# An order of its own for the first eight slots of an attention and feed-forward kernel

## The reference

```python
q, k, v = (x @ Wk.T + bk), (ctx @ Wk.T + bk), (ctx @ Wv.T + bv)      # per head
s  = q k' / sqrt(32)
p  = softmax(where(allow, s, -1e32));  cum = cumsum(p)
eff = clip(exp(sqrt(clip((total - cum) * |i - j|, 0)) * -softplus(gamma)), 1e-5, 1e5)
a  = softmax(where(allow, s * eff, -1e32)) @ v
x1 = layernorm(x + a @ Wo.T + bo)
out = layernorm(x1 + relu(x1 @ W1.T + b1) @ W2.T + b2)               # 512 -> 2048 -> 512
```

## Time and profile before

| | |
|---|---|
| median of 3 runs | 1585.5 us (1583.85 to 1588.65) |
| the profiled execution | 1583.35 us |
| its span, first to last instruction | 1581.6 us |
| busy | PE 1489.3, weight loads 1234.4, DVE 1129.6, ACT 1038.3, POOL 108.1 us |
| mean granted TensorE clock | 0.976 |
| moved by DMA | 334 MB, 211 GB/s |

### The profile page before, as it was taken

One profiled execution on the slowest core, in us unless ns is written; L12 is line 12 of the kernel. 1 busy time (PEld: TensorE's weight loads), 2 busy tenths in 40 slices (PEclk: granted clock), 3 DMA queues, 4 the chain that ended last, 5 costly groups with the idle time before them and its releaser, 6 DMA issues.

```text
span 1581.6 us, 34611 instructions
## 1 busy us (share of the span) xinstructions
PE 1489.3 (94%) x13056; PEld 1234.4 (78%) x13056; DVE 1129.6 (71%) x3843; ACT 1038.3 (66%) x2677; POOL 108.1 (7%) x96
## 2 busy tenths in 40 slices
PE   4577899999999999999999999999999999999897
PEld 3455788888888888888888888888888888887786
DVE  5788668687776868777686877768687776867433
ACT  2777666766666676666667666666766666676522
POOL 4000101000010100100010010101000000100000
PEclk8778999999999999999999999999999999999999
DMA  6775455565655556565555656555565655555676
GB/s 213 249 244 218 182 187 202 201 216 197 216 209 200 204 201 220 191 225 201 200 204 199 222 192 225 201 201 206 200 223 190 223 202 201 206 200 202 245 281 251
DMA packets 62773, 334.12 MB, mean 211 GB/s; under 512 B 8208, under 2 KB 8208, under 8 KB 29456
## 3 DMA queue, kind: packets, MB, share of 16 engines
q1 hardware_dynamic: 62608, 331.92, 58.9%
HBM read 306.72 MB, written 25.17 MB: 210 GB/s over the span
## 4 chain that ended last, share of the span: by engine, by line
PE 64%; DVE 24%; ACT 8%; issue 2%; POOL 1%; DMA 0%; SPq 0%; DVEq 0%; POOLq 0%; ACTq 0%
PE bank L199 18%; PE bank L200 16%; PE bank L201 16%; PE bank L385 7%; DVE w_sb L925 5%; DVE w_sb L913 5%; PE bank L399 4%; DVE w_sb L935 2%; DVE gz L921 2%; ACT w_sb L637 1%; ACT w_sb L639 1%; ACT w_sb L635 1%; DVE s_sb L901 1%; PE bank L419 1%; DVE rows L988 1%
## 5 line engine op out<-in xcount | busy, mean ns | idle before, releaser
L199 PE MATMUL bank<-xt_hi,w_ring 128*128 128x256 f32 x1024 | 296.9, 290 | 2.3 <-ACT h_sb L708 2.3
L201 PE MATMUL bank<-xt_hi,w_ring 128*128 128x256 f32 x1024 | 288.9, 282 | 0.0
L200 PE MATMUL bank<-xt_lo,w_ring 128*128 128x256 f32 x1024 | 288.6, 282 | 0.0
L901 DVE CUSTOM_DVE_ANT_0 s_sb<-bank,mask 128x256 f32<-128x256 f32 (+7 forms) x512 | 130.1, 304 | 184.0 <-PE bank L385 182.2
L658 ACT COPY pt_sb<-bank 128x512 f32<-128x512 f32 x192 | 111.9, 583 | 200.1 <-PE bank L399 200.1
L628 ACT ACTIVATE w_sb<-s_sb,nm 128x161 f32<-128x161 f32 (+7 forms) x512 | 164.3, 404 | 87.9 <-DVE nm L909 87.9
L199 PE MATMUL bank<-w_ring,h_hi 128*128 128x512 f32 x512 | 210.9, 412 | 9.6 <-DVE h_lo L1000 9.6
L648 ACT ACTIVATE p_sb<-w_sb,nm 128x32 f32<-128x32 f32 (+7 forms) x512 | 205.6, 405 | 0.0
L201 PE MATMUL bank<-w_ring,h_lo 128*128 128x512 f32 x512 | 203.2, 397 | 0.0
L200 PE MATMUL bank<-w_ring,h_hi 128*128 128x512 f32 x512 | 203.1, 397 | 0.0
L199 PEld LDWEIGHTS bank<-xt_hi,w_ring 128*128 128x128 f32 x1024 | 193.5, 189 | 9.1 <-issue 5.9
(11 more groups left out here) (120 smaller groups left out, 2961.3 us busy)
## 6 DMA issues: line engine op xcount, KB each, us to landing
w_ring<-w_split SPq DMA_DIRECT2D x256, 1024.0 KB, 4.9
w_split<-w_ring SPq DMA_DIRECT2D x32, 512.0 KB, 5.4
x_raw<-x_t SPq DMA_DIRECT2D x16, 512.0 KB, 4.0
c_raw<-ctx_t SPq DMA_DIRECT2D x16, 512.0 KB, 5.0
u_sb<-x_rows SPq DMA_DIRECT2D x16, 512.0 KB, 6.4
ring_raw<-w SPq DMA_DIRECT2D x32, 256.0 KB, 5.5
out<-rows SPq DMA_DIRECT2D x16, 512.0 KB, 6.9
wk_raw<-wk SPq DMA_DIRECT2D x1, 1024.0 KB, 4.8
```

The source lines that it names most:

```text
L199: nc.tensor.matmul(dst, a_hi, b_hi, start=start, stop=False)
L200: nc.tensor.matmul(dst, a_hi, b_lo, start=False, stop=False)
L201: return nc.tensor.matmul(dst, a_lo, b_hi, start=False, stop=stop)
L901: m = nc.vector.tensor_tensor_reduce(out=s_sb[:, c % 2, W_AT[b] + 1:W_AT[b] + 1 + WIDTH[b]], in0=s_bank[n % 2][:, at:at + WIDTH[b]], in1=m ...
```

## The change

The first eight slots (batches 0 and 1, steps 0 and 1 up to the start of step 2) get a function `first()` on every engine, with its own order; from step 2 on, `step` is as before. In `first()`:

- DVE empties all three parts of the scores of a slot before `decayed_scores` of the slot before it; before, the third part came after. `totals` stands ahead of both, the splits stand after `running_sums`.
- V of batches 0 and 1 (`values`) and the second half of the first product with Wo go to `y_bank`, which nothing else uses yet; both halves of V, and both halves of the product with Wo, stand together. The product with Wo follows `concat(0, 3)`, which DVE now has after the splits of slot 5.
- The high parts of W1 and W2 are cast by POOL and no longer by ACT. Blocks are split in the order 4 to 15, then 0 to 3 (`SPLIT`); slots 1 to 6 take 2, 3, 2, 3, 3 and 3 blocks (`SPLIT_BY`). Blocks 0 to 3 stay in `w_ring`, whose places are laid out anew, and the first loads of two pairs fall away.
- SP issues `x_in` and `c_in` after the stores of slots 2 and 6, where before it did so before the stores of slot 2.
- The first waits are finer: `wk` is split in a part of 128 columns and the rest, `bk` has a semaphore of its own, the gammas are loaded from ACT's queue, DVE waits for the mask alone at first, PE for nothing until its first transposes; POOL makes the mask first.

```diff
-        def over_batches(step):
-            for i in range(B + 3):
-                step(i, i < B, 1 <= i <= B, 2 <= i <= B + 1, 3 <= i, i + 1 < B)
+        def over_batches(first, step):
+            first()
+            for i in range(2, B + 3):
+                step(i, i < B, i <= B, i <= B + 1, 3 <= i, i + 1 < B)
+        SPLIT = [*range(4, FT), *range(4)]
+        SPLIT_BY = (0, 2, 5, 7, 10, 13, 16, 16)
         def split_in(n):
-            return range(3 * n, 3 * n + 3) if n < 4 else range(2 * n + 4, 2 * n + 6) if n < 6 else ()
+            return range(SPLIT_BY[n - 1] if n else 0, SPLIT_BY[n])
...
-            def raw_hidden(f):
+            def raw_hidden(at):
+                f = SPLIT[at]
                 n = f % 4
-                if f >= 4:
-                    sp.wait_ge(split_out[n], 32 * (f // 4))
-                sp.dma_start(ring_raw[:, 2 * n, 1], w1[:, f].rearrange("p k m -> p (k m)")).then_inc(raw_in[n], 16)
-                sp.dma_start(ring_raw[:, 2 * n + 1, 1], w2[:, f]).then_inc(raw_in[n], 16)
-            def store_hidden(f):
+                if at >= 4:
+                    sp.wait_ge(split_out[n], 32 * (at // 4))
+                sp.dma_start(ring_raw[:, n, 1], w1[:, f].rearrange("p k m -> p (k m)")).then_inc(raw_in[n], 16)
+                sp.dma_start(ring_raw[:, 4 + n, 1], w2[:, f]).then_inc(raw_in[n], 16)
+            def store_hidden(at):
+                f = SPLIT[at]
                 n = f % 4
-                sp.wait_ge(ffw_lo_ok, f + 1)
+                sp.wait_ge(ffw_lo_ok, at + 1)
                 sp.dma_start(w1_split[f // 2, :, f % 2],
-                             w_ring[:, 2 * n].bitcast(F32).rearrange("p n m -> p (n m)")).then_inc(split_out[n], 16)
+                             w_ring[:, n].bitcast(F32).rearrange("p n m -> p (n m)")).then_inc(split_out[n], 16)
                 sp.dma_start(w2_split[f // 2, :, f % 2],
-                             w_ring[:, 2 * n + 1].bitcast(F32).rearrange("p n m -> p (n m)")).then_inc(split_out[n], 16)
+                             w_ring[:, 4 + n].bitcast(F32).rearrange("p n m -> p (n m)")).then_inc(split_out[n], 16)
...
-            sp.dma_start(bk_col[:], bk).then_inc(col_in, 16)
+            sp.dma_start(bk_col[:], bk).then_inc(bk_in, 16)
             with nc.allow_non_contiguous_dma(reason="short vectors, once"):
-                for h in range(HQ):
-                    sp.dma_start(g_in[R * h:R * h + R, :],
-                                 gammas.rearrange("(c h) -> h c", h=HQ)[h].partition_broadcast(R)).then_inc(col_in, 16)
                 raw_weight(1, wv_raw, wv)
...
+            def first():
+                for n in range(2 * NQ):
+                    for at in split_in(n):
+                        store_hidden(at)
+                        if 1 <= at and at + 3 < FT:
+                            raw_hidden(at + 3)
+                    if n == 2:
+                        sp.wait_ge(qk_mm, NQ)
+                        sp.wait_ge(v_mm, RT)
+                        x_in(1)
+                        c_in(1)
+                    if n == 6:
+                        sp.wait_ge(qk_mm, 2 * NQ)
+                        sp.wait_ge(v_mm, 2 * RT)
+                        x_in(2)
+                        c_in(2)
+                    if n == 7:
+                        sp.wait_ge(x1_ok, RT)
+                        sp.dma_start(u_sb[:], x_by_batch[1]).then_inc(xrow_in, 16)
+                        for m in range(4):
+                            sp.wait_ge(split_out[m], 32 * (FT // 4))
+                        w1_behind(0, 0)
+                        w1_behind(0, 1)
+                        w2_behind(0, 0)
...
-                    if NQ * i + c == 5:
-                        for n in range(4):
-                            sp.wait_ge(split_out[n], 32 * (FT // 4))
-                        for p in range(2):
-                            w1_pair(p)
-                            w2_pair(p)
...
-            def values(i, t):
+            def values(i, t, to=pj_bank):
...
-                pe.wait_ge(w1_in[p % 2], 16 * ((NP // 2) * i + p // 2 + 1))
+                if g < 2:
+                    pe.wait_ge(ffw_lo_ok, FT - 2 + 2 * p)
+                else:
+                    pe.wait_ge(w1_in[p % 2], 16 * ((NP // 2) * i + p // 2))
...
-                pe.wait_ge(w2_in[p % 2], 16 * ((NP // 2) * i + p // 2 + 1))
+                if g >= 2:
+                    pe.wait_ge(w2_in[p % 2], 16 * ((NP // 2) * i + p // 2))
...
+            def first():
+                scores(0, 0, 0)
+                scores(0, 0, 1)
+                scores(0, 0, 2)
+                pe.wait_ge(qk_ok, 1)
+                pe.wait_ge(wk_lo_ok, 2)
+                queries_keys(0, 1)
+                scores(0, 1, 0)
+                scores(0, 1, 1)
+                scores(0, 1, 2)
+                pe.wait_ge(qk_ok, 2)
+                queries_keys(0, 2)
+                values(0, 0, y_bank[0])
+                values(0, 1, y_bank[1])
+                scores(0, 2, 0)
+                scores(0, 2, 1)
+                pe.wait_ge(const_ok, CONSTS)
+                transposes(0, 0, 0)
+                scores(0, 2, 2)
+                pe.wait_ge(qk_ok, 3)
+                queries_keys(0, 3)
+                transposes(0, 0, 1)
+                transposes(0, 0, 2)
+                attend(0, 0)
+                scores(0, 3, 0)
+                scores(0, 3, 1)
+                transposes(0, 1, 0)
+                scores(0, 3, 2)
+                transposes(0, 1, 1)
+                transposes(0, 1, 2)
+                pe.wait_ge(qk_ok, 4)
+                queries_keys(1, 0)
+                attend(0, 1)
+                pe.wait_ge(v_ok, 2)
+                values(1, 0, y_bank[0])
+                values(1, 1, y_bank[1])
+                scores(1, 0, 0)
+                scores(1, 0, 1)
+                transposes(0, 2, 0)
+                scores(1, 0, 2)
+                pe.wait_ge(qk_ok, 5)
+                queries_keys(1, 1)
+                transposes(0, 2, 1)
+                transposes(0, 2, 2)
+                attend(0, 2)
+                scores(1, 1, 0)
+                scores(1, 1, 1)
+                transposes(0, 3, 0)
+                scores(1, 1, 2)
+                pe.wait_ge(qk_ok, 6)
+                queries_keys(1, 2)
+                transposes(0, 3, 1)
+                transposes(0, 3, 2)
+                attend(0, 3)
+                pe.wait_ge(qk_ok, 7)
+                pe.wait_ge(v_ok, 4)
+                project_rows(0, 0)
+                project_rows(0, 1, y_bank[1])
+                scores(1, 2, 0)
+                scores(1, 2, 1)
+                transposes(1, 0, 0)
+                scores(1, 2, 2)
+                pe.wait_ge(u_ok, 1)
+                queries_keys(1, 3)
+                transposes(1, 0, 1)
+                transposes(1, 0, 2)
+                turn_rows(0, 0)
+                attend(1, 0)
+                scores(1, 3, 0)
+                scores(1, 3, 1)
+                turn_rows(0, 1)
+                transposes(1, 1, 0)
+                scores(1, 3, 2)
+                hidden(0, 0)
+                transposes(1, 1, 1)
+                transposes(1, 1, 2)
+                pe.wait_ge(qk_ok, 8)
+                queries_keys(2, 0)
+                hidden(0, 1)
+                attend(1, 1)
+                pe.wait_ge(qk_ok, 9)
+                values(2, 0)
+                add_hidden(0, 0)
...
-            pe.wait_ge(const_ok, CONSTS)
-            over_batches(step)
+            over_batches(first, step)
...
-            def split_high(f):
-                n = f % 4
-                act.wait_ge(raw_in[n], 32 * (f // 4 + 1))
-                nc.scalar.copy(w_ring[:, 2 * n:2 * n + 2, 0],
-                               ring_raw[:, 2 * n:2 * n + 2, 1]).then_inc(ffw_hi_ok, 1)
...
+            def first():
+                first_exp(0, 0)
+                weight_high(2, wo_hi, wo_raw)
+                qk_copy(0, 1)
...
+                effect(0, 0)
+                first_exp(0, 1)
+                qk_copy(0, 2)
+                second_exp(0, 0, 0)
+                second_exp(0, 0, 1)
+                value_rows(0, 0, y_bank[0])
+                value_rows(0, 1, y_bank[1])
...
+                effect(0, 2)
+                turned(0, 1, 0)
+                concat_high(0, 0)
+                first_exp(0, 3)
+                turned(0, 1, 1)
+                second_exp(0, 2, 0)
+                turned(0, 1, 2)
+                second_exp(0, 2, 1)
+                qk_copy(1, 0)
+                reciprocals(0, 1)
+                value_rows(1, 0, y_bank[0])
+                value_rows(1, 1, y_bank[1])
...
+                effect(1, 0)
+                turned(0, 3, 0)
+                concat_high(0, 2)
+                first_exp(1, 1)
+                turned(0, 3, 1)
+                qk_copy(1, 2)
+                second_exp(1, 0, 0)
+                turned(0, 3, 2)
+                second_exp(1, 0, 1)
+                reciprocals(0, 3)
+                concat_high(0, 3)
...
```

(109 more changed lines are left out.)

142 lines of the change are left out of this document (85 added, 57 removed).

## The result

The changed kernel takes 1595.12 us (median of 5 runs, 1593.54 to 1595.30), the kernel before 1585.5 us (1583.61 to 1588.65). The ratio is 1.0061, with a 95% interval of 1.0048 to 1.0074: slower by 0.6%, +9.6 us. The forecast was +5.1 us, with a chance of 0.48 for "slower" by more than 0.3%. Direction and range were right, the size was about half of what came. The profiled execution after took 1593.54 us, its span is 1591.7 us, 10.1 more than before: 8.7 of it at the start of step 2, 1.4 behind it.

The account below looks back on a forecast made before the run. DVE was taken to set the pace of the slots before step 2, PE after it. Slot terms put step 2 at 188.3 instead of 183.2 us, +5.1, so 1590.6 us, range 1580 to 1601.

Parts of the forecast that it names:

- The yardstick: From step 2 on, code unchanged and PE-bound: 1398.4 us carried over, so only the start of step 2 counts.
- T0: Start of the scan in slot 0 (T0 to T7 for slots 0 to 7): forecast 22 us, before 32.2.
- three waits go: Before the first scan: wk's low part about 2 us, PE's wait for POOL's constant 3.4, V between scores 4.6.
- at no cost: Two first pairs left in place, gammas loaded from ACT's queue and finer semaphores were to cost nothing.
- T0 to T1: First to second scan: 13.8 us of DVE work plus 2.5 for POOL, second scan at 38.2 us.
- The term for POOL: First to second scan: POOL's first four casts and two adds beside DVE cost it 2.5 us.
- The first wait: Slot before the fourth scan: DVE stands 10.6 us for x_hi of batch 1, issued behind stores; slot 31 us.
- The second wait: Slot before the seventh scan: late concat(0, 3) delays the Wo product and then scores; slot 31.4 us, before 18.8.
- T6 to T7: Seventh to eighth scan: 22.1 us, eighth scan at 174.5, with `x_in(2)` hidden behind stores without loads.
- The sum: Step 2 at 188.3 us instead of 183.2: +5.1 us, 1590.6 us as median.
- Rival 2: POOL takes its full price: 16 casts at 1.04 us, mostly on DVE's path, +14 us, 1600; chance 0.13.
- Rival 1: Batch 1's inputs land in time, so the 10.6 us wait goes: balance -5.5, 1580 us; chance 0.19.

Follow-up runs that it names:

- experiment 2: The kernel before, with SyncE issuing x and c of batch 1 behind the stores of slot 2: 1595.95 us, ratio 1.0071.
- Experiment 7: The changed kernel with ScalarE waiting for the masks and 16 small constants, not all of POOL's constants: 1592.72 us, one run.
- experiment 1's second kernel: The changed kernel with batch 1's inputs ahead of slot 2's stores on SyncE and ahead of POOL's casts of blocks 5 to 7: 1587.0 us, ratio 1.0009.
- experiment 1's first: The changed kernel with SyncE issuing x and c of batch 1 ahead of the stores of slot 2: 1593.95 us, one run.
- experiment 5: The changed kernel with all 16 casts of weights on ScalarE instead of POOL: 1589.42 us, ratio 1.0029.
- experiment 1: The changed kernel with batch 1's inputs ahead of slot 2's stores on SyncE: 1593.95 us; then also ahead of POOL's casts of blocks 5 to 7: 1587.0 us.
- Experiments 3 and 4: The changed kernel: 3, Wo product behind all scores of slot 6 on TensorE, 1591.09 us; 4, concat(0, 3) ahead of slot 5's splits on VectorE, 1591.31 us.
- experiment 8: The changed kernel with SyncE issuing x and c of batch 2 ahead of the stores of slot 6: 1595.6 us, one run.
- experiment 9: The changed kernel with VectorE masking the third part of the scores behind `decayed_scores` in slots 1 to 7, as before: 1604.61 us, one run.
- all_fixed: The changed kernel with batch 1 and 2 inputs, concat(0, 3), two thirds of slot 6's scores and ScalarE's constants wait all moved earlier: 1576.32 us, ratio 0.9949.

## Why the prediction was right in kind and half in size

- *The yardstick.* The time behind step 2 was to be 1398.4 us and is 1399.8. In the profiles of the experiments on the changed kernel it is 1398.9 to 1399.9, in experiment 2 1398.7. The 1.4 us are a real but small miss of "unchanged"; 1.0 of them falls behind the last scan, and the cause stays open.
- *T0*, forecast 22, came at 25.6. The step that failed is "three waits go". Those did, but a wait of the same kind took their place on ScalarE: `first_exp` needs the last constant, POOL's `ident`, and stood 3.9 us for it. The forecast followed PE's wait for POOL, not ACT's. Experiment 7 gets 1.9 us of it back. Some 1.3 us of the wait is a collision: POOL's `ident` took 1.54 us beside the low part of wk, against 0.29 before. Where `ident` itself was spared, a smaller instruction ahead of it was hit and T0 did not move (experiment 1's second kernel: 1.57 us for 0.20, T0 25.8); in the one profile without experiment 7's edit where all of them up to `ident` were spared (experiment 1's first) T0 was 24.1. Another 0.8 us lies in the loads at the start, which the prediction put "at no cost". Here is x's first cast before, then after, with x issued at 1.17 us in both:

```profile
6.91 1.04 POOL L1148 CAST x_hi<-x_raw 128x1024 fp32r<-128x1024 f32 x1 [3.16 <-DMA x_raw<-x_t]
```

```profile
8.55 1.04 POOL L1415 CAST x_hi<-x_raw 128x1024 fp32r<-128x1024 f32 x1 [3.94 <-DMA x_raw<-x_t]
```

  It begins 8.55 to 8.88 us into the span in the changed kernel and every variant of it, and PE began 1.2 us earlier (10.99 for 12.21) where the sum had 2. Whether the two loads of wk, the gammas on ACT's queue or the earlier load of wv delay it, no run shows; the last us or so of the miss was not followed.
- *T0 to T1*, forecast 16.2, took 18.4. The term for POOL was 2.5 us and measured 4.45 on the products alone (experiment 5). The price per us of POOL was about right, 0.8 for the forecast's 0.72 (0.75 for a cast of 1.04); wrong was that only two thirds of it would meet such work. T1 to T2, without POOL, took 13.6 against 14.4: the costs per slot were right.
- *The first wait.* Forecast 10.6 us for x_hi and a slot of 31, measured 9.3 and 29.8. The size was right and half of the cause was missing: SyncE's order was named, but POOL's own, with x behind three weight casts that each wait for a load, holds x almost as long (81.0 for 82.6, experiment 1). The prediction counted POOL's casts as a price for DVE and never as a queue in front of x. Who had acted on it would have moved SyncE's line and gained nothing that one run can tell.
- *The second wait.* Forecast 31.4 us for the slot, measured 31.2, with the named chain: PE 7.09 us idle before Wo, DVE 8.1 us before the scores. Experiments 3 and 4 show it from both ends.
- *T6 to T7*, forecast 22.1, took 25.2. "`x_in(2)` ... is hidden" was off by 0.93 us, and the sum had no term for POOL in this stretch: 2.2 us for the add (experiment 8) and 0.8 for x's cast, beside which the maxima took 0.95 us for 0.17. T7 to step 2 took 11.6 us for 13.8.
- *The sum.* Start 3.6, T0 to T1 2.2 and T6 to T7 3.1 too little, the other stretches together 5.3 too much: 3.6 us at step 2. So step 2 was as near as it was by errors that partly cancel. 1.4 us more came behind step 2. The terms for POOL were low, and so was the start. One reading of the rows was off too: PE is busy 10.2 to 15.9 us of the slots shown in the earlier trace rows, not 13 to 16; no term rests on it. Rival 2, POOL's full price, gave 14 us and lay as far off on the other side; +9.6 is about midway. The Trainium skill's rule ("GPSIMD Engine Reference", Key points) that POOL contends with VectorE's instructions of two inputs agrees with 6.77 us for 2.32. It names 2-port modes too; the runs show one-input instructions stretched as well, the clip to 1.59 us for 0.73, and do not show in which mode these ran.
- *Rival 1*, inputs in time, is what experiment 1's second kernel builds: it lies at 1587.0, ratio 1.0009, where the rival said 1580. T5 to T6 took its 31.2 us as in the sum; the start, slot 0 and T6 to T7 were too low in the rival's sum as in the forecast's, by 9.1 us in this profile (25.8, 18.3 and 25.3 us for 22, 16.2 and 22.1), and slot 2 took 22.3 for 20.5.

Where the gain went: the scans were 6.6 us ahead at T0, 10.6 at T1 and 14.4 at T2. x behind two queues took 10.8 us of that back at T3 (3.6 ahead). At T5 they were 10.5 ahead; the slot with the Wo product took 31.2 us for 18.8, so they were 1.9 behind at T6. T6 to T7 cost 5.3 more, with three splits in a slot that had none before:

```profile
160.42 3.49 DVE L1091 TENSOR_TENSOR w_ring<-ring_raw,w_ring 128x1024 fp32r<-128x1024 f32 x3
```

T7 to step 2 cost the last 1.5. Without the new order within the slot step 2 would be 12 us later still (experiment 9, one run).

## What to carry to other kernels

When several queues get an order of their own, follow each new consumer through every queue that it passes: here x passed SyncE's stores and POOL's casts. Moving SyncE's line alone left VectorE 8.1 us of the 9.3 us wait, taking the casts off POOL alone left 10.8, and both together left none: two causes of one wait must be removed together. Waits in different slots added up: experiments 1, 3, 4 and 7 brought 6.0, 1.5, 2.5 and 0.9 us at step 2, together 10.9 (experiment 8 brought none), and `all_fixed` 12.6. Put an in-order engine's work for others (the small `concat`, 2.5 us here) ahead of its bulk work.

## What the runs showed of the hardware that was not expected

- A VectorE instruction that meets a POOL operation can last as long as that operation, however small its own work: 128x32 decayed scores 2.36 us for 0.19, eight negated maxima 0.95 for 0.17, beside POOL operations of 2.62 and 1.04 us.
- It stretches POOL too: the 128x128 `affine_select` 1.54 us for 0.29, and x's high part 3.23 us for 1.04 in experiment 8.
- In these rows the one that begins second is the one that gets longer, by about what the first has left. The two VectorE instructions began 0.31 and 0.12 us behind POOL's and ended with it. The `affine_select` began 0.36 us behind VectorE's low part of wk and ended 0.15 us after it; x's high part began 0.17 us behind a scan of 2.56 us and ended 0.84 us after it. This is read off four meetings; no run varied the order by itself.
